# A gated-linear-attention chunk loop, worked through in two halves of the heads instead of step by step over all heads

## The reference

```python
q, k, v = heads(h @ Wq), heads(h @ Wk), heads(h @ Wv)
gk = log_sigmoid(h @ Wgk1 @ Wgk2 + bgk2) / 16
# per chunk of tokens, state S carried from chunk to chunk:
b = cumsum(gk)                       # over the tokens of the chunk
q_g, k_intra, k_state = q*exp(b)*scale, k*exp(-b), k*exp(b_last - b)
scores = tril(q_g @ k_intra.T)
o = scores @ v + q_g @ S
S = S * exp(b_last) + k_state.T @ v
o = o * rsqrt(mean(o*o) + eps) * g_norm_w * silu(h @ Wg)
out = o @ Wo
```

## Time and profile before

| what | value |
|---|---|
| median of the 2 runs shown | 5336.89 us (5297.4 and 5376.39) |
| the profiled execution, slowest core | 5196.89 us |
| its span in the trace, core 3 | 5195.4 us |
| spans of the 8 cores | 5159.9 to 5195.4 us |
| mean granted TensorE clock per core | 0.760 to 0.766 |
| busy in the span: PE, DVE, ACT | 2912.5, 1454.5, 806.4 us |

### The profile page before, as it was taken

How to read it: one execution, slowest core, us unless ns; L and a number is a source line. 1 busy time by engine, 2 the same in 40 slices (tenths; PEclk the granted TensorE clock), 3 DMA queues, 4 the chain that set the end, 5 groups by cost and what they waited for, 6 DMA issues and landing times.

```text
span 5195.4 us, 41234 instructions; the slowest of 8 cores (5159.9 to 5195.4 us)
## 1 busy us (share of the span) xinstructions
PE 2912.5 (56%) x13392; PEld 1299.8 (25%) x13392; DVE 1454.5 (28%) x2709; ACT 806.4 (16%) x1517; POOL 175.6 (3%) x279
## 2 busy tenths in 40 slices
PE   0123454554455315555445555657567977788777
PEld 0001222222222102222222222223223433343333
DVE  0122343243334333343434342242421011100111
ACT  0000210121021002111210211211211122112211
POOL 1000000000000000000000000000000000000000
PEclk9866676766777657677667667779678988899888
DMA  9623103201210242032013102104023333333332
GB/s 112 94 76 110 51 19 117 101 13 73 101 57 13 99 160 91 17 113 99 25 65 113 61 13 96 71 13 152 13 97 140 125 127 140 130 126 133 138 130 89
DMA packets 107262, 456.62 MB, mean 88 GB/s; under 512 B 28065, under 2 KB 40369, under 8 KB 71202
## 3 DMA queue, kind: packets, MB, share of 16 engines
q1 hardware_dynamic: 40050, 268.74, 14.7%
q0 software_dynamic: 67008, 185.24, 12.2%
HBM read 411.99 MB, written 75.50 MB: 94 GB/s over the span
## 4 chain that ended last, share of the span: by engine, by line
PE 50%; DVE 17%; DMA 12%; issue 9%; ACT 7%; another core or an unknown queue 4%; DVEq 1%; ACTq 0%; POOL 0%; POOLq 0%; SPq 0%
PE po L996 9%; PE pq L966 9%; PE pr L871 5%; DMA x2f<-Wfc 5%; PE pq L635 4%; PE pq L653 4%; DMA x2f<-Wpj 2%; PE pq L588 2%; PE pq L604 2%; PE po L833 2%; DVE xT L858 2%; DVE qfp L446 2%; DMA xtm<-xin 2%; PE po L837 2%
## 5 line engine op out<-in xcount | busy, mean ns | idle before, releaser
L966 PE MATMUL pq<-qf,meg 128*128 128x512 bf16 x2048 | 496.0, 386 | 10.8 <-DVE za L952 8.3
L996 PE MATMUL po<-meg 128*128 128x512 bf16 x2048 | 452.4, 379 | 7.6 <-DVE z2a L984 7.6
L635 PE MATMUL pq<-meg,xT 128*128 128x512 bf16 x1024 | 245.3, 405 | 288.2 <-DMA meg<-wv_s 269.1
L458 PE MATMUL pt<-id,qbf 128*128 128x128 bf16 x512 | 59.9, 290 | 536.6 <-DVE qbf L453 536.6
L871 PE MATMUL pr<-meg,xT 128*128 128x512 bf16 x1024 | 280.8, 443 | 69.7 <-DVE xT L858 69.7
L439 ACT ACTIVATE sgn<-x2f 128x512 bf16<-128x512 f32 x128 | 80.6, 630 | 1272.7 <-DMA x2f<-Wfc 623.0
L966 PEld LDWEIGHTS pq<-qf,meg 128*128 128x128 bf16 x2048 | 202.0, 99 | 268.6 <-issue 37.6
L996 PEld LDWEIGHTS po<-meg 128*128 128x128 bf16 x2048 | 199.8, 98 | 251.1 <-issue 11.4
L653 PE MATMUL pq<-meg,xT 128*128 128x512 bf16 x1024 | 239.0, 396 | 22.4 <-ACT meg L657 11.8
L561 PE MATMUL pq<-idf,xtm 128*128 128x128 f32 x256 | 54.4, 371 | 312.0 <-DMA xtm<-xin 302.4
L974 ACT ACTIVATE meg<-pq,cols 128x512 bf16<-128x512 f32 x256 | 175.5, 687 | 305.2 <-PE pq L970 305.1
(11 more groups left out here) (183 smaller groups left out, 3731.3 us busy)
## 6 DMA issues: line engine op xcount, KB each, us to landing
meg<-wfc_s SPq DMA_DIRECT2D x64, 1024.0 KB, 4.8
meg<-wpj_s SPq DMA_DIRECT2D x64, 1024.0 KB, 4.8
x2f<-Wfc POOLq DMA_DIRECT2D x64, 512.0 KB, 4.1
meg<-wv_s SPq DMA_DIRECT2D x32, 1024.0 KB, 5.1
meg<-wg_s SPq DMA_DIRECT2D x32, 1024.0 KB, 7.3
meg<-wo_s SPq DMA_DIRECT2D x32, 1024.0 KB, 7.1
x2f<-Wpj POOLq DMA_DIRECT2D x16, 2048.0 KB, 8.3
meg<-wq_s SPq DMA_DIRECT2D x16, 1024.0 KB, 7.0
```

The source lines that it names most:

```text
L458: (lambda e, kk=kk, pbuf=pbuf: e.transpose(out=pt[:, kk * 128:(kk + 1) * 128], in_=pbuf[:, kk * 128:(kk + 1) * 128], identity=id128[:]))
L635: ems.append(lambda e, pb=pb, wsl=wsl, rc=rc, kk=kk, j=j: e.matmul(out=pb[:], lhsT=xT[:, kk * 512 + j * 128:kk * 512 + (j + 1) * 128], rhs ...
L966: ems.append(lambda e, pb=pb, slot=slot, o4=o4, kk=kk: e.matmul(out=pb[:], lhsT=slot[:, o4 * 1024 + kk * 128:o4 * 1024 + (kk + 1) * 128], ...
L996: ems.append(lambda e, pb=pb, slot=slot, kk=kk: e.matmul(out=pb[:], lhsT=slot[:, kk * 128:(kk + 1) * 128], rhs=h1[:, kk * 512:(kk + 1) * 512],
```

## The change

Only the chunk loop changes. Its steps from the gate to `xT` are put inside one loop `for hb in range(2)`, where hb 0 is heads 0 and 1 and hb 1 is heads 2 and 3. In detail:

- Keys are split by half: `spf0/1`, `sphl0/1`, `eqc0/1`, `ekc0/1`, `erc0/1`, `qg0/1`, `ki0/1`, `kt0/1`, `pu0/1`, `scm0/1`, `og0/1`, `diagd0/1`. The buffers stay as they are.
- 1024-wide operations become two of 512: the `Ln`, the cast and the subtraction to `sphl`, `qg`, `ki`, both on `kt`. The decay `Exp` becomes two of 4 columns, the rms `Ln` and `Exp` two of 2.
- The totals go to `pr0` and `pr1` instead of `pu`.
- Outputs use only po0 and po1, two heads at a time; `pq0` and `pq1` hold no outputs any more.
- Each half writes its rms factor, its `og`, its four state updates, its eight transposes and its four `xT` writes before the next half begins.
- `pend` is let out after half 0's `xT` writes, instead of after `ekc`.
- The output projection and the layer norm stay behind both halves.

The diff, cut; the lines of half 0 and half 1 are the same with `hb` 0 and 1, and of the removed lines only the head is shown:

```diff
             pend = []
             for c in range(4):
-                for half in range(2):
-                    bank = "pq0" if half == 0 else "pq1"
...
                 for hb in range(2):
...
+                    gb = "pq0" if hb == 0 else "pq1"
+                    gp = halves[gb]
+                    sph = "sphl%d" % hb
+                    P.mm_group([lambda e, gp=gp, hb=hb, c=c: e.matmul(
...
+                        start=True, stop=True)], rd=["t1a", "wgk2a"], wr=[gb])
+                    P.op("scalar", lambda e, gp=gp, hb=hb: e.activation(
+                        out=spf[:, hb * 512:(hb + 1) * 512], in_=gp[:],
+                        func=AF.Exp, scale=-1.0), rd=[gb], wr=["spf%d" % hb])
+                    P.op("scalar", lambda e, hb=hb: e.activation(
+                        out=spf[:, hb * 512:(hb + 1) * 512],
+                        in_=spf[:, hb * 512:(hb + 1) * 512], func=AF.Ln, bias=1.0),
+                        rd=["spf%d" % hb], wr=["spf%d" % hb])
+                    P.op("vector", lambda e, hb=hb: e.tensor_copy(
+                        out=sphl[:, hb * 512:(hb + 1) * 512],
+                        in_=spf[:, hb * 512:(hb + 1) * 512]),
+                        rd=["spf%d" % hb], wr=[sph])
+                    P.op("vector", lambda e, hb=hb: e.tensor_sub(
+                        sphl[:, 1024 + hb * 512:1024 + (hb + 1) * 512],
+                        spf[:, hb * 512:(hb + 1) * 512],
+                        sphl[:, hb * 512:(hb + 1) * 512]),
+                        rd=["spf%d" % hb, sph], wr=[sph])
...
+                    P.mm_group(ems, rd=[sph, "Ub"], wr=[gb])
+                    db = "pr0" if hb == 0 else "pr1"
+                    dp = halves[db]
+                    ems = []
...
+                    P.mm_group(ems, rd=[sph, "ones1"], wr=[db])
+                    P.op("scalar", lambda e, dp=dp, hb=hb: e.activation(
+                        out=cols[:, C_DC + 4 * hb:C_DC + 4 * hb + 4], in_=dp[:, 0:4],
+                        func=AF.Exp, scale=-1.0 / 16.0), rd=[db], wr=["cols"])
+                    for d4 in range(4):
+                        dd = hb * 4 + d4
+                        P.op("vector", lambda e, dd=dd: e.tensor_scalar(
+                            out=diagd[:, dd * 128:(dd + 1) * 128], in0=id128[:],
+                            scalar1=cols[:, C_DC + dd:C_DC + dd + 1], op0=ALU.mult,
+                            scalar2=None), rd=["id128", "cols"], wr=["diagd%d" % hb])
...
                     P.mm_group([
...
+                        (lambda e, gp=gp, hb=hb: e.matmul(
+                            out=gp[:], lhsT=Lb[:], rhs=sphl[:, hb * 512:(hb + 1) * 512],
                             start=True, stop=False)),
...
+                    P.op("scalar", lambda e, gp=gp, hb=hb: e.activation(
+                        out=erc[:, hb * 512:(hb + 1) * 512], in_=gp[:], func=AF.Exp),
+                        rd=[gb], wr=["erc%d" % hb])
...
+                    P.op("vector", lambda e, c=c, hb=hb: e.tensor_tensor(
+                        out=e3(ki, hb), in0=kv3[:, 4 * hb:4 * hb + 4, c * 128:(c + 1) * 128],
+                        in1=e3(ekc, hb), op=ALU.mult),
+                        rd=["kfb", "ekc%d" % hb], wr=["ki%d" % hb])
                     P.mm_group([
...
+                        (lambda e, kk=kk, c=c: e.transpose(
+                            out=pt[:, kk * 128:(kk + 1) * 128],
+                            in_=kfm[:, kk * 512 + c * 128:kk * 512 + (c + 1) * 128],
+                            identity=id128[:]))
+                        for kk in range(4 * hb, 4 * hb + 4)], rd=["kfb", "id128"], wr=["pt"])
+                    P.op("vector", lambda e, hb=hb: e.tensor_copy(
+                        out=kt[:, hb * 512:(hb + 1) * 512],
+                        in_=pt[:, hb * 512:(hb + 1) * 512]), rd=["pt"], wr=["kt%d" % hb])
...
+                            for d in range(2)],
+                            rd=["ki%d" % hb, "qg%d" % hb], wr=["pu%d" % hb])
+                        P.op("vector", lambda e, h=h: e.tensor_mul(
+                            scm[:, h * 128:(h + 1) * 128], pu[:, h * 128:(h + 1) * 128],
+                            mskT[:]), rd=["pu%d" % hb, "mskT"], wr=["scm%d" % hb])
+                    for h in (2 * hb, 2 * hb + 1):
+                        bank = "po0" if h % 2 == 0 else "po1"
+                        pb = halves[bank]
...
+                        P.mm_group(ems, rd=["scm%d" % hb, "qg%d" % hb, "vt%d" % c,
+                                            "S%d" % (2 * h), "S%d" % (2 * h + 1)],
+                                   wr=[bank])
+                        P.op("scalar", lambda e, pb=pb, h=h: e.activation(
+                            out=sqs[:, 0:512], in_=pb[:], func=AF.Square,
+                            accum_out=cols[:, C_SSQ + h:C_SSQ + h + 1]),
+                            rd=[bank], wr=["sqs", "cols"])
+                    P.op("scalar", lambda e, hb=hb: e.activation(
+                        out=cols[:, C_R + 2 * hb:C_R + 2 * hb + 2],
+                        in_=cols[:, C_SSQ + 2 * hb:C_SSQ + 2 * hb + 2],
+                        func=AF.Ln, scale=1.0 / 512.0, bias=cols[:, C_EPS:C_EPS + 1]),
+                        rd=["cols"], wr=["cols"])
+                    P.op("scalar", lambda e, hb=hb: e.activation(
+                        out=cols[:, C_R + 2 * hb:C_R + 2 * hb + 2],
+                        in_=cols[:, C_R + 2 * hb:C_R + 2 * hb + 2],
+                        func=AF.Exp, scale=-0.5), rd=["cols"], wr=["cols"])
...
+                    for h in (2 * hb, 2 * hb + 1):
+                        for d in range(2):
+                            sb = "po0" if (h * 2 + d) % 2 == 0 else "po1"
+                            pb = halves[sb]
+                            sk = "S%d" % (2 * h + d)
+                            dd = 2 * h + d
+                            P.mm_group([
...
+                                rd=["diagd%d" % hb, "kt%d" % hb, "vt%d" % c, sk],
+                                wr=[sb])
+                            P.op("vector", lambda e, pb=pb, dd=dd: e.tensor_copy(
+                                out=St[:, dd * 512:(dd + 1) * 512],
+                                in_=pb[:]), rd=[sb], wr=[sk])
+                    g2 = hb
...
-                        for b in range(8)], rd=["og", "id128"], wr=["pt"])
+                        for b in range(8)], rd=["og%d" % hb, "id128"], wr=["pt"])
...
-                if STAGE < 10:
-                    continue
+                    if hb == 0:
+                        while pend:
+                            pend.pop(0)()
                 for oh in range(2):
                     bank = "pr0" if oh == 0 else "pr1"
                     pb = halves[bank]
```

More of the change, by code:

```diff
@@ L720, in build_program @@
-                P.mm_group(ems, rd=["sphl", "ones1"], wr=["pu"])
-                P.op("scalar", lambda e: e.activation(
-                    out=cols[:, C_DC:C_DC + 8], in_=pu[:, 0:8], func=AF.Exp,
-                    scale=-1.0 / 16.0), rd=["pu"], wr=["cols"])
-                for dd in range(8):
-                    P.op("vector", lambda e, dd=dd: e.tensor_scalar(
-                        out=diagd[:, dd * 128:(dd + 1) * 128], in0=id128[:],
-                        scalar1=cols[:, C_DC + dd:C_DC + dd + 1], op0=ALU.mult,
-                        scalar2=None), rd=["id128", "cols"], wr=["diagd"])
@@ L738, in build_program @@
[L738 to L741, removed]
-                for half in range(2):
-                    bank = "pq0" if half == 0 else "pq1"
-                    pb = halves[bank]
+                    P.mm_group(ems, rd=[sph, "Ub"], wr=[gb])
+                    db = "pr0" if hb == 0 else "pr1"
+                    dp = halves[db]
+                    ems = []
+                    for kk4 in range(4):
+                        kk = hb * 4 + kk4
+                        ems.append(lambda e, dp=dp, kk4=kk4, kk=kk: e.matmul(
+                            out=dp[:, kk4:kk4 + 1],
+                            lhsT=sphl[:, kk * 128:(kk + 1) * 128],
+                            rhs=ones1[:], start=True, stop=False))
+                        ems.append(lambda e, dp=dp, kk4=kk4, kk=kk: e.matmul(
+                            out=dp[:, kk4:kk4 + 1],
+                            lhsT=sphl[:, 1024 + kk * 128:1024 + (kk + 1) * 128],
+                            rhs=ones1[:], start=False, stop=True))
@@ new lines, in build_program @@
+                    P.op("scalar", lambda e, gp=gp, hb=hb: e.activation(
+                        out=eqc[:, hb * 512:(hb + 1) * 512], in_=gp[:], func=AF.Exp,
+                        bias=cols[:, C_NLN16:C_NLN16 + 1]),
+                        rd=[gb, "cols"], wr=["eqc%d" % hb])
+                    P.op("scalar", lambda e, gp=gp, hb=hb: e.activation(
+                        out=ekc[:, hb * 512:(hb + 1) * 512], in_=gp[:], func=AF.Exp,
+                        scale=-1.0), rd=[gb], wr=["ekc%d" % hb])
@@ L845, in build_program @@
-                if STAGE < 9:
```

(9 more changed lines are left out.)

174 lines of the change are left out of this document (50 added, 124 removed).

## The result

The changed kernel is slower: its median is 5435.12 us (5401.92 to 5574.19, 11 runs) against 5276.03 us for the kernel before (5194.71 to 5376.39, 10 runs, the two shown ahead of the prediction among them). The ratio is 1.0386, with a 95% interval of 1.0334 to 1.0438. Some executions of most kernels here, and all six of e_onekey, ran with a lower granted clock on some of the cores and took up to 6% longer; the medians hold them, the ratios leave them out. The profiled executions took 5401.92 and 5196.89 us, a difference of 205 us; the forecast was +185 us, +3.5%, on a base of 5337.

The account below looks back on a forecast made before the run. No engine fills a chunk of about 52 us; a chain of hand-overs between engines bounds it. 24 x 6.5 + 8 x 3.6 = +185 us on the 5337 us median gave 5522 us, range 5400 to 5640.

Parts of the forecast that it names:

- The order: Chunk loop: engine queues keep half 1 from starting under half 0, making two serial half-chains; 5522 us, chance 0.70.
- The half-chain: One half's steps from `Exp` through its tail: 24.0 us for half 0, 22.0 for half 1, 45.9 together against 38.60.
- to first mask: Decay `Exp` to first masked score in a half: 3.97 us, running over ScalarE, where before took 6.51.
- to `og`: First output matmul through the rms factor to `og` in a half: 4.35 us for two heads, before 6.21 for four.
- to `og` transposes: A half's state updates up to its `og` transposes: 3.6 us, where eight updates took 8.23 before.
- tail: Transposes to the next `Exp` in half 0, 4.6 us with `pend`; transposes to the output projection in half 1, 3.0.
- The signs: Trace marks: halves' `Exp` 23 to 25 us apart, chunk 58 to 60, projection to next `Exp` 12 to 14, FFN unchanged.
- the term of before: Old kernel's `Exp` to projection, read as 38.60 and 40.1 us in two chunks; middle taken, giving +6.5 per chunk.
- A: Rival, faster: half 1's front runs under half 0's back in the chunk loop; 200 us less, 5137 us; chance 0.05.
- B: Rival, no difference: each half-chain is some 2 us shorter than estimated, below +3 per chunk, 5400 us; chance 0.10.
- C: Rival, slower by more: TensorE's clock falls, lengthening state, output and projection matmuls; 2.7 us more per chunk, 5608 us; chance 0.15.
- The base: Starting time of the whole kernel: median 5336.9 us of the two runs shown, onto which +185 us was put.

Follow-up runs that it names:

- e_onekey: e_inter, but with one dependence key per buffer for both halves: 5445.06 to 5624.12 us in six executions, no ratio; the same kernel run again gave 1.0245 of before.
- e_inter: The changed kernel's split pieces, each step written for half 0 then half 1, in the order of the kernel before: 5210.49 us, 1.000 of before.
- e_warm: The changed kernel plus four 512-column matmuls per half behind the output matmuls, result unused: 1.0306 of before.
- e_pipe3: e_pipe with next chunk's transposes and scores grouped, `pend` and next gate behind outputs and rms, next sums to `erc` behind the state: 4863.32 us, 0.9322 of before.
- e_pipe: e_inter with the next chunk's whole front, gate to `kt`, spread over the present chunk: 5093.75 us, 0.9784 of before.

## Why the prediction was right

**The order.** The text said that the new keys allow overlap and the queues forbid it. The timeline after shows it, and e_inter showed it by itself: the same pieces, interleaved, are back at 1.000.

**The half-chain.** Step by step, in us, for the chunk at 1164.22; half 1's front from the same timeline, its end from the rows above.

| step | predicted | half 0 | half 1 |
|---|---|---|---|
| `Exp` to cast | 1.85 / 1.45 | 1.73 | 1.42 |
| cast to cumulative sum | 1.59 | 1.61 | 1.76 |
| to decay `Exp` | 1.36 | 1.35 | 1.35 |
| to first mask | 3.97 | 4.07 | 4.07 |
| to first output | 1.54 | 1.52 | 1.52 |
| to `og` | 4.35 | 4.35 | 4.35 |
| to state | 1.11 | 1.13 | 1.11 |
| to `og` transposes | 3.6 | 3.40 | 3.82 |
| tail | 4.6 / 3.0 | 4.42 | 2.74 |
| sum | 24.0 / 22.0 | 23.58 | 22.14 |

Together 45.72 us up to the projection, where the sum had 45.9. From there to the next `Exp` it is 12.85 us, against 12.57.

**The signs.** Over all chunks of the slowest core half 1's `Exp` comes 23.87 us after half 0's (forecast 23 to 25) and 21.31 in chunk 0 (about 21); half 1's `Exp` to the projection is 22.4 us (about 22), the pitch 59.32 (58 to 60), projection to next `Exp` 13.09 (12 to 14), and the FFN stage kept its length.

**The terms.** From the `Exp` to the projection it is +7.30 us in chunks 1 to 3 and +4.04 in chunk 0, where the forecast had +6.5 and +3.6. 24 x 7.30 + 8 x 4.04 = 207 us, against 205.0 between the two spans. The two half-chains were sized well, 45.9 against 46.23. What was mis-sized is the term of before: the prediction read 38.60 us from one chunk and 40.1 from its neighbour, and took the middle, 39.35, where the mean of the 24 is 38.93. The first reading, +7.3, was right, and averaging it with a chunk longer than most made it 0.8 too low. One or two chunks were too few for a mean. So the shortfall needs no clock: the steps were priced at this trace's durations, and the priced steps came out within 0.4 us. A lower clock is in the measured 46.23 all the same, as e_warm shows; how it is shared between the steps is open.

**The rivals.** A did not happen: no overlap of the halves exists in the trace after. Its rule isn't borne out by a run here either. The Trainium skill, "Perfetto Trace Analysis", section "Optimizing Scalar/DVE Operations", says that breaking up instructions may allow work to be completed sooner if VectorE or ScalarE cause bubbles. In this case the broken up instructions gave 1.000 interleaved, which is no gain, and 1.0386 end to end; e_pipe3, where the order gives each engine something to do in the other's time, gave 0.932, and none of the runs tells what splitting adds to that. B fell with the table above. C came in part: the granted clock of a chunk fell from 0.70 to 0.64, under its mark of 0.66, but the projection, its larger term, didn't lengthen (8.88 us in the mean against 8.78, where it wanted over 10).

**The clock.** The granted clock of the stretch before half 1's `Exp`, in which TensorE is busy 11.12 of 23.58 us, is 0.57, and of the rest, where it is busy 18.96 of 34.99 us and has the long projection, 0.68. With that agrees the Trainium skill, "TensorE: Matmul & The Clock Gate", section "What's actually happening": the slow state is the default and activity releases it.

**The base.** 5522 us stood against 5435.12, which is 87 too high. 61 of it is the base, since the eight further runs brought the median of before to 5276.03; the other 26 is the difference, 159 us between the medians where 185 stood. On the profiled executions the difference is 205, so there the 185 was 20 low. That the time fell inside 5400 to 5640 is helped by errors of opposite sign and by the width of the range. The ratio, 1.035 against 1.0386, is the sounder comparison.

**Where a price was off.** Moving `pend` alone cost the kernel before 2.7 us a chunk, not 1.5, and moving it back gave 3.4, not 2.5.

## What to carry to other kernels

A dependence key, or a smaller tile, only says what may overlap; each engine's queue says what will. Before a loop is closed around a whole chain, look up for each engine what stands ahead of the second iteration's first instruction, and what that waits for. A chain bound by hand-overs gets shorter by writing the next iteration's front into the waits of this one (here 0.932 of the time), and each piece must stand where its input is ready, or it blocks the queue: e_pipe and e_pipe3 differ by nothing else but order and grouping, and by 4.7% of the time (0.9784 and 0.9322).

## What was not expected of the hardware

Added TensorE work can shorten a kernel: 4 matmuls of 512 columns per half-chunk, 256 in all, with an unused result, made the changed kernel about 0.8% faster (1.0306 and 1.0386 of before; the intervals just meet, at 1.0334), while 256 of them in the kernel before made it 0.3% slower. The granted clock over the execution went from 0.733 to 0.756 with them in the one, and from about 0.764 to 0.769 in the other.
